# Rotary query products of five quads of heads: seven half-size block products in place of eight full ones

## The reference, cut to what matters

```
q = (x @ wq).reshape(b, s, H, QH)          # H = 16, QH = 128 + 64
q_nope, q_pe = (q[..., :NOPE], q[..., NOPE:])
q_pe = _rope(q_pe, cos, sin)               # 64 columns a head
scores = einsum(concat(q_nope, q_pe), concat(k_nope, k_pe)) * scale, causal
attn = softmax(scores);  out = attn @ v @ wo
```

## Time and profile before

| | us |
|---|---|
| median of 3 runs | 1493.23 (1492.83 to 1495.04) |
| the profiled execution, its own time | 1490.77 |
| its span in the profile | 1489.0 |
| PE busy | 1458.8 (98%) |
| DVE / ACT / POOL busy | 1036.4 / 1013.8 / 1039.1 |

### The profile page before, as it was taken

How to read it: one execution, slowest core, us unless ns; L and a number is a source line. 1 busy time by engine, 2 the same in 40 slices (tenths; PEclk the granted TensorE clock), 3 DMA queues, 4 the chain that set the end, 5 groups by cost and what they waited for, 6 DMA issues and landing times.

```text
span 1489.0 us, 27368 instructions
## 1 busy us (share of the span) xinstructions
PE 1458.8 (98%) x8340; PEld 794.8 (53%) x8340; DVE 1036.4 (70%) x2627; ACT 1013.8 (68%) x2581; POOL 1039.1 (70%) x1087
## 2 busy tenths in 40 slices
PE   6999999999999999999999999999999999999998
PEld 5544555554555545555555555555555555555664
DVE  7877787877777766665656565656656666676887
ACT  7877778777877586667556676666656666654664
POOL 3689787876776588676658866567656876674664
PEclk9999999999999999999999999999999999999999
DMA  6599989898888588787958777886785787864664
GB/s 203 150 195 206 209 185 199 191 187 165 160 172 166 129 155 188 137 190 144 202 109 154 154 137 148 167 158 151 162 194 110 141 163 154 154 160 105 149 146 111
DMA packets 652257, 240.53 MB, mean 162 GB/s; under 512 B 599889, under 2 KB 614737, under 8 KB 651729
## 3 DMA queue, kind: packets, MB, share of 16 engines
q1 hardware_dynamic: 652112, 238.79, 77.3%
HBM read 75.10 MB, written 20.97 MB: 65 GB/s over the span
## 4 chain that ended last, share of the span: by engine, by line
PE 88%; ACT 3%; DVE 3%; POOL 3%; issue 2%; DMA 1%; SPq 0%; POOLq 0%; DVEq 0%; ACTq 0%
PE ps L642 17%; PE ps L644 17%; PE ps L643 17%; PE ps L846 7%; PE ps L852 7%; PE ps L851 7%; PE ps L847 7%; PE ps L848 7%; POOL st L1899 2%; ACT ex L1131 1%; DVE ps L1553 1%; ACT st L1141 0%; DMA acc<-x_in 0%; PE ps L675 0%; DVE acc L1604 0%
## 5 line engine op out<-in xcount | busy, mean ns | idle before, releaser
L1899 POOL TENSOR_TENSOR st<-ex,st 128x512 f16<-128x512 f32 (+3 forms) x640 | 638.3, 1018 | 376.0 <-ACT st L1141 367.8
L1131 ACT ACTIVATE ex<-ps,nm,scales 128x512 f32<-128x512 f32 (+3 forms) x640 | 453.0, 711 | 400.6 <-DVE nm L1570 391.2
L1551 DVE TENSOR_REDUCE gm<-ps 128x1 f32<-128x512 f32 (+1 forms) x384 | 250.3, 671 | 193.8 <-PE ps L852 188.9
L1141 ACT ACTIVATE st<-ex 128x512 f16<-128x512 f32 (+3 forms) x640 | 343.1, 563 | 5.4 <-ACT ex L1131 0.4
L846 PE MATMUL ps<-kTh,q 128*128 128x512 f16 (+3 forms) x640 | 222.3, 347 | 6.9 <-ACT ex L1131 4.3
L642 PE MATMUL ps<-pT,vH 128*128 128x512 f16 (+3 forms) x640 | 222.1, 347 | 1.7 <-DMA pT<-st 1.7
L1604 DVE SCALAR_TENSOR_TENSOR acc<-ps,rden,acc 128x512 f32<-128x512 f32 x256 | 189.6, 745 | 46.8 <-PE ps L644 45.9
L851 PE MATMUL ps<-kRh,q 128*128 128x512 f16 (+3 forms) x640 | 222.2, 347 | 0.0
L852 PE MATMUL ps<-kRl,q 128*128 128x512 f16 (+3 forms) x640 | 222.1, 347 | 0.0
L848 PE MATMUL ps<-kTh,q 128*128 128x512 f16 (+3 forms) x640 | 222.1, 347 | 0.0
L847 PE MATMUL ps<-kTl,q 128*128 128x512 f16 (+3 forms) x640 | 222.1, 347 | 0.0
(11 more groups left out here) (320 smaller groups left out, 2486.6 us busy)
## 6 DMA issues: line engine op xcount, KB each, us to landing
wS<-w_abs SPq DMA_DIRECT2D x48, 256.0 KB, 3.2
wV<-w_vo SPq DMA_DIRECT2D x48, 256.0 KB, 2.9
pT<-st SPq DMA_TRANSPOSE x640, 3.3
wS<-w_abs SPq DMA_DIRECT2D x24, 384.0 KB, 3.4
fland<-factors_in SPq DMA_DIRECT2D x28, 256.0 KB, 3.0
wP<-w_pe SPq DMA_DIRECT2D x24, 256.0 KB, 3.2
wsq<-wq_in SPq DMA_DIRECT2D x16, 256.0 KB, 3.8
wso<-wo_in SPq DMA_DIRECT2D x16, 256.0 KB, 3.1
```

Source lines behind the costliest of these rows:

```text
L1131: e.activation(ex[:, n % NEX, 0:keys], s_bank(n)[:, 0:keys], ACT.Exp, bias=nm[:, (i * QT + r) % 4:(i * QT + r) % 4 + 1], scale=scales[:, p ...
L1141: e.activation(stage(n, keys)[:, :, 0, :], ex[:, n % NEX, 0:keys].rearrange("p (t n) -> p t n", n=P), ACT.Copy).then_inc(z["a_pH"], 1)
L1551: e.tensor_reduce(m, b, AX_X, ALU.max).then_inc(z["v_max"], 1)
L1899: e.tensor_tensor(s[:, :, 1, :], ex[:, n % NEX, 0:keys].rearrange("p (t n) -> p t n", n=P), s[:, :, 0, :], ALU.subtract).then_inc(z["g_pL" ...
```

## The change

The rotary products of the twenty units 28 to 47 (five quads of heads, `QUADS` = 28, 32, 36, 40, 44) are no longer made pair by pair. For a quad, a 512-feature by 256-column weight and a 512-token chunk make a product of two-by-two blocks of 256, and that is done by seven block products: `r1`, `r6`, `r2`, `r5`, `r7`, `r3`, `r4`. Each is two times three matmuls of 256 columns into half a PSUM bank. VectorE reads each bank alone, once or twice, into sums in fp32 that stand in the free part of `pT` (`rope_read`, eight instructions a quad), and `rot` then reads these sums in place of a PSUM bank. The sums and differences of token blocks are those that the non-rotary products already use. The weights' sums are made from the stored weights `w_pe` on GpSimd (14 instructions) and ScalarE (4), once for each of four groups of heads, in nine slots each from (17, 2), (19, 2), (26, 1) and (28, 2) on; they are stored to a new DRAM tensor `w_quad` and loaded for each quad. The products of a quad that begins at unit e stand in slots (e - 6, 0), (e - 6, 2), (e - 6, 3), (e - 4, 0), (e - 4, 2), (e - 4, 3) and (e - 3, 3). `rot` moves from (e - 2, 0) to (e - 3, 2). Units under 28 and from 48 on keep their products as they were. Several of VectorE's semaphores are merged into one, `v_own`, to make room for new ones.

```diff
+FIRST_QUAD = H + 12
+LAST_PASS = (NC - 1) * H
+QUADS = tuple(range(FIRST_QUAD, LAST_PASS, 4))
+R_STEPS = ("r1", "r6", "r2", "r5", "r7", "r3", "r4")
+R_READS = ("s1", "u", "c11", "v", "c22", "u2", "c12", "c21")
+R_LAST = {"r1": "s1", "r6": "u", "r2": "c11", "r5": "v", "r7": "u2", "r3": "c12", "r4": "c21"}
+R_BLOCK = {"r1": (0, 0), "r2": (0, 1), "r6": (2, 1), "r5": (2, 0), "r3": (2, 3), "r7": (2, 2), "r4": (1, 0)}
...
+def quad_slots(e):
+    u = e - 6
+    return {"r1": (u, 0), "r6": (u, 2), "r2": (u, 3), "r5": (u + 2, 0), "r7": (u + 2, 2), "r3": (u + 2, 3), "r4": (u + 3, 3)}
...
+R_SUMMED = tuple(e % H // 4 for e in QUADS[:4])
+R_SUMS = {}
+for n, first in enumerate(((H + 1, 2), (H + 3, 2), (H + 10, 1), (H + 12, 2))):
+    R_SUMS[n] = [divmod(first[0] * 4 + first[1] + s, 4) for s in range(9)]
+R_LOADS = ((H + 1, 0), (H + 3, 0), (H + 8, 0), (H + 11, 3))
+G_SUMS, A_SUMS = 6 * (H // 2), 4 * (H // 2)
...
+def rot_at(x):
+    return (x - 3, 2) if by_quad(x) else (x - 2, 0 if x <= LAST_PASS else 3)
+def turn_at(x):
+    return (x - 2, 2) if x <= (NC - 1) * H else (x - 1, 0)
...
+    rotary = [(step, e) for e in QUADS for step, at in quad_slots(e).items() if at == (i, r)]
...
-        if H <= i <= (NC - 1) * H - 2 and i % 2 == 0:
-            out.append(("pe", i + 2))
+        if i % 2 == 0 and (H < i + 2 < FIRST_QUAD or i + 2 == LAST_PASS):
+            out += rotary + [("pe", i + 2)]
+        else:
+            out += rotary
...
+    if r:
+        out += rotary
...
-IN_BANKS = ("q", "pe", "tkv", "wvo", "tq", "wabs", "out", "ffn", "m1", "m2", "m7")
+IN_BANKS = ("q", "pe", "tkv", "wvo", "tq", "wabs", "out", "ffn", "m1", "m2", "m7") + R_STEPS
...
+            def rope_block(step, x):
+                n, k = QUADS.index(x), x // H
+                o = free_bank((step, x))
+                load = {"r1": "d_ra", "r6": "d_rs", "r4": "d_rb"}
+                if step in load:
+                    e.wait_ge(z[load[step]], 16 * (n + 1))
+                if x % H == 0 and step == "r1":
+                    e.wait_ge(z["d_xT"], 32 * k)
+                if x % H == 0 and step in ("r6", "r7", "r4"):
+                    e.wait_ge(z["g_tok"], 4 * k - 2 + ("r6", "r7", "r4").index(step))
+                part, at = R_BLOCK[step]
+                w = w_quad[part] if part == 1 else w_quad[part][:, at, :, :]
+                token = {"r1": (0, 0), "r2": (1, 0), "r3": (1, 1)}
+                for m in range(2):
+                    rhs = [token_block(k, a, *token[step])[:, m, :] if step in token else
+                           summed(k, {"r6": 2, "r5": 1, "r7": 3, "r4": 4}[step], a)[:, m, :] for a in range(2)]
+                    ins = three(o[:, 0:HC], [w[:, a, m * P:(m + 1) * P] for a in range(2)], rhs, m == 0, m == 1)
+                ins.then_inc(z["p_r"], 1)
...
+            def rope_sums_high(n, step):
+                s, f, ops = {2: (0, 0, 3), 3: (1, 1, 5), 5: (3, 2, 8), 7: (2, 0, 12)}[step]
+                e.wait_ge(z["g_sum"], G_SUMS + 14 * n + ops)
+                if step == 2:
+                    e.wait_ge(z["g_tok"], 4 if n < 2 else 8)
+                    if n:
+                        e.wait_ge(z["d_sS"], 16 * (H // 2 + n))
+                e.activation(r_made[:, s, 0, :], r_tmp[f], ACT.Copy).then_inc(z["a_sum"], 1)
...
+            def rope_read(step, x):
+                c11, c12 = rope_of[0][:, 0:HC], rope_of[0][:, HC:CH]
+                c21, c22 = rope_of[1][:, 0:HC], rope_of[1][:, HC:CH]
+                o = bank((step, x))[:, 0:HC]
+                e.wait_ge(z["p_r"], made_r(step, x))
+                if step == "r1":
+                    if x == FIRST_QUAD:
+                        e.wait_ge(z["p_pv"], H)
+                    e.tensor_copy(c11, o).then_inc(z["v_r"], 1)
+                    return
+                for to, add, behind in {"r6": ((rope_u, c11, "s1"),), "r2": ((c11, c11, "s1"),), "r5": ((c12, rope_u, "u"),),
+                                        "r7": ((c22, c12, "v"), (c21, rope_u, "u")), "r3": ((c12, c12, "v"),),
+                                        "r4": ((c21, c21, "u2"),)}[step]:
+                    e.wait_ge(z["v_r"], read_r(behind, x))
+                    e.tensor_tensor(to, o, add, ALU.add).then_inc(z["v_r"], 1)
...
-                b = bank(("pe", i))
+                if not by_quad(i):
+                    b = bank(("pe", i))
+                    e.wait_ge(z["p_pe"], pe_number(i) + 1)
+                else:
+                    b = rope_of[i % 4 // 2]
+                    e.wait_ge(z["v_r"], read_r("c21" if i % 4 else "c12", i - i % 4))
...
+            def rope_sums(n, step):
+                t0, t1, t2 = r_tmp
+                elif step == 4:
+                    put(t2, h12, t1, sub, behind=5)
+                    put(t2, t2, l12, add, behind=7)
+                    put(r_made[:, 1, 1, :], t1, r_made[:, 1, 0, :], sub, high=2)
...
+            def load_rope(kind, x):
+                n, q = QUADS.index(x), x % H // 4
+                left = {"ra": "r2", "rs": "r3", "rb": "r4"}[kind]
+                if n:
+                    e.wait_ge(z["p_r"], made_r(left, x - 4))
+                else:
+                    e.wait_ge(z["p_pv"], H - 1)
+                if kind == "ra":
+                    e.dma_start(w_quad[0].rearrange("p b a n -> p a b n"),
+                                wP_d[2 * q].rearrange("p a (b n) -> p a b n", b=2)).then_inc(z["d_ra"], 16)
+                elif kind == "rb":
+                    e.dma_start(w_quad[1], wP_d[2 * q + 1, :, :, HC:CH]).then_inc(z["d_rb"], 16)
+                else:
+                    if n < H // 4:
+                        e.wait_ge(z["d_sS"], 16 * (H // 2 + n + 1))
+                    e.dma_start(w_quad[2], wR_d[q]).then_inc(z["d_rs"], 16)
...
-                    if r == (2 if i < H else 0) and i % 2 and H <= i + 3 < NU:
+                    if r == (2 if i < H else 0) and i % 2 and H <= i + 3 < NU and not by_quad(i + 3):
                         load_pe(i + 3)
-                    if r == 1 and h == H - 3 and k + 1 < NC:
+                    for n in R_SUMS:
+                        if (i, r) == R_LOADS[n]:
+                            load_pairs(n)
+                        if (i, r) == R_SUMS[n][-1]:
+                            store_rope_sums(n)
+                    for lead in QUADS:
+                        for kind, at in (("ra", (lead - 9, 0)), ("rs", (lead - 7, 0)), ("rb", (lead - 6, 1))):
+                            if (i, r) == at:
+                                load_rope(kind, lead)
```

More of the change, by code:

```diff
@@ L275, in fills @@
             out += [("pe", e), ("rot", e), ("turn", e)]
-        if H < e <= (NC - 1) * H and (i, r) == (e - 2, 0):
+        if e > H and (i, r) == rot_at(e):
+            if e > LAST_PASS:
+                out += [("den", i - 1)] * (i > LAST_PASS) + [("pe", e)]
             out.append(("rot", e))
[L278 to L282, removed]
+        if e > H and (i, r) == turn_at(e):
             out.append(("turn", e))
@@ L326, in fills @@
         out.append(("wf", KEPT.index((i, r))))
+    for n in R_SUMS:
+        out += [("rsum", (n, s)) for s in range(9) if R_SUMS[n][s] == (i, r)]
     for k in range(1, NC):
@@ L507, in build @@
         wP_d = nc.dram_tensor("w_pe", [H // 2, P, 2, E], F16).ap()
+        wR_d = nc.dram_tensor("w_quad", [H // 4, P, 4, 2, HC], F16).ap()
         xT_d = nc.dram_tensor("x_t", [NC - 1, P, 2 * KE, CH], F16).ap()
@@ L651, in left @@
                 user = used_before[key]
-                if user and user[0] == "s":
+                if user and user[0] in R_LAST:
+                    e.wait_ge(z["v_r"], read_r(R_LAST[user[0]], user[1]))
+                elif user and user[0] == "s":
                     e.wait_ge(z["a_exp"], user[1] + 1)
@@ L1280, in _ @@
         def _(e):
[L1281 removed]
+            chained, made = itertools.count(1), {}
             def own():
@@ L1788, in sums_low, with put @@
                 e.tensor_tensor(weight_block(at, 1), f, weight_block(at, 0), ALU.subtract).then_inc(z["g_sum"], 1)
+            def rope_sums(n, step):
+                t0, t1, t2 = r_tmp
+                (h11, l11), (h12, l12) = [[pair_a[:, b, a, :] for a in range(2)] for b in range(2)]
+                (h21, l21), (h22, l22) = [[pair_b[b][:, a, :] for a in range(2)] for b in range(2)]
+                add, sub = ALU.add, ALU.subtract
+                def put(to, f, g, op, behind=0, high=0):
+                    if behind:
+                        e.wait_ge(z["g_sum"], G_SUMS + 14 * n + behind)
+                    if high:
+                        e.wait_ge(z["a_sum"], A_SUMS + 4 * n + high)
+                    e.tensor_tensor(to, f, g, op).then_inc(z["g_sum"], 1)
+                if step == 0:
+                    e.wait_ge(z["d_rp"], 48 * (n + 1))
+                    if n:
+                        e.wait_ge(z["g_sum"], G_SUMS + 14 * n)
+                    if n == 0:
+                        e.wait_ge(z["p_tkv"], H + 3)
+                        e.wait_ge(z["p_wvo"], H)
```

(22 more changed lines are left out.)

99 lines of the change are left out of this document (77 added, 22 removed).

## The result

The changed kernel is slower: 1498.18 us in the median (1497.44 to 1499.79, 6 runs) against 1492.87 us of the kernel before in the same session; the ratio is 1.0038, 95% interval 1.0025 to 1.0051. The forecast was 1490.1 us, 0.2% faster. The profiled execution took 1498.41 us with a span of 1495.4, so the span grew by 6.4 us where 3.1 less were forecast.

A forecast was written before the change was run, and what follows sets the result against it. A full TensorE queue was taken as the bound. Matmuls -2.9 us and `m6` -0.2, the rest at 0, sum to -3.1, taking the median from 1493.23 to 1490.1 us; range 1488.4 to 1493.3.

The forecast's parts named there:

- Shorter slots: Slots 0 of units 26 to 44 lose rotary matmuls; exponentials, values and banks still fit: cost 0, bound +1 us.
- The sentence on banks: A block product's bank is asked for again at the earliest by the same slot's `out`, in (22, 0) and (24, 0).
- The matmul term: Five quads: 42 matmuls of 256 columns, 0.1094 us each, replace 24 of 512; 0.58 us a quad, 2.92 saved.
- The term of `m6`: Ahead of `m6`: waits gone in five units, -1.0 us, longer in 19 and 21, +0.8; net -0.2 us.
- VectorE, GpSimd, ScalarE, SyncE at nothing: Added reads, `rot` from SBUF, weights' sums and loads cost 0; upper bounds +3 us for `rot`, +2 for GpSimd, ScalarE, SyncE.
- The slower one by GpSimd: GpSimd late in units 17 to 21 and 26 to 30, TensorE standing in eight slots 0: 1499 us; chance 0.06.
- The rival of the weight loads: The 90 added weight loads cost their 98 ns instead of staying hidden: +8.8 us, 1499 us; chance 0.01.
- The sign named for the profile: In the profile after, PE busy in units 16 to 47 is down by 3 us.

The follow-up runs named there:

- the first: Changed kernel with the output product of slot 0 in even units 26 to 44 moved to slot 1, ahead of that slot's own: 1488.98 us, ratio 0.9983.
- fourth: Kernel of the first experiment with the feed-forward product put ahead of the rotary block in the slots they share: 1487.58 us, ratio 0.9973.
- the sixth: Kernel of the fourth experiment with the weights' sums begun one slot later: 1487.82 us, ratio 0.9979.
- the fifth: Kernel before the change, with the output products of slot 0 in even units 26 to 44 moved to slot 1: 1491.87 us, ratio 1.0003.

## Why the prediction was wrong

**The step that failed is "Shorter slots".** It put the cost of taking 1.93 us out of slot 0 at 0, with a bound of +1, after looking at the exponentials, the values and the banks. The first two were judged rightly, since neither waits; the banks come below. What it never asked is what the next instruction of TensorE itself needs: the output product behind the removed matmuls, whose operand VectorE makes in the same slot. The measured cost is 8.47 us. All that was needed were two rows for each slot, VectorE's read and the start of `out`. The smallest spare of the ten, 0.23 us in (32, 0), was in the trace, and so was the same wait come true in (48, 0), 1.08 us; I had the earlier trace rows with 912.31 in it and took it as the end of a stretch of matmuls rather than as a reader. The odd units' slots were as close (0.2 us) and unharmed, as nothing was taken there.

**The sentence on banks in the same step failed too.** It held that a block product's bank is asked for again at the earliest by `out` in (22, 0) and (24, 0). It looked at who follows a block product, and not at whom the shifted rotation puts behind `out`: +0.87 us in (37, 3).

**The matmul term was right.** Over the whole trace the distance from a matmul of the new blocks to the next start, where nothing is waited for, is 0.1093 us in the mean of 201, at the clock of 1.00; forecast were 0.1094. With the output products in the same places the measured gain is 3.0 us, to about 1.8 either way, which agrees with the 2.92 and the small terms around it. By the Trainium skill's "TensorE: Matmul & The Clock Gate", section "Back-to-back issue gap", the same exchange would lose about 4.8 us, the prediction's estimate from that page. The trace does not agree: the 90 added weight loads are in it, and the matmuls stand 0.109 us apart.

**The term of `m6` was right in its places and nearly in each size**: five waits gone, two of 0.54 where 0.64 were forecast. Summed they give -0.5 us, forecast -0.2.

**VectorE, GpSimd, ScalarE, SyncE at nothing were right in the sum.** `rot` out of SBUF was slower than the lower bound, three groups of VectorE after:

```profile
L1678 DVE TENSOR_TENSOR rot<-pT,tab 64x512 f32<-64x512 f32 x10 | 12.5, 1252 | 0.1
L1677 DVE TENSOR_TENSOR rot<-pT,tab 64x512 f32<-64x512 f32 x10 | 11.9, 1190 | 0.1
L1676 DVE TENSOR_TENSOR rot<-pT,tab 128x512 f32<-128x512 f32 x10 | 7.7, 766 | 0.0
```

Together 3.21 us in the mean, between the bounds of 2.06 and 4.6. The ten differ, from 2.06 to 3.78 us, and five of them take 3.77 or 3.78, more than the 3.19 us of slack: there, and once at 3.37, the next maximum starts with no idle time of VectorE ahead of it. No wait of TensorE came of it, as the step had argued. The timeline shows what goes with the long ones: the four of the thirty instructions with no GpSimd instruction beside them take 0.68 or 0.69 us, and all of over 1 us have GpSimd busy for 0.6 us or more of their time. The run without the weights' sums shows GpSimd's and ScalarE's to cost nothing beyond the two waits of `m6`.

**The rivals.** The slower one by GpSimd named 1499 us and the kernel took 1498, but its mechanism did not happen: GpSimd's and ScalarE's added work taken away gives back only the 0.6 us at `m6`. The rival of the weight loads named 1499 too, and the distance of 0.1093 us speaks against it. That both numbers came near is luck. The rival had the right form, a cover of about 1 us used up in many slots, at the wrong reader. The chance of slower, 0.07, came almost all (0.06) from that one mechanism, since the step for shorter slots had been closed as safe. The sign named for the profile, PE busy in units 16 to 47 down by 3 us, came out at 7.8 (684.5 to 676.7): what lies beyond the matmuls is TensorE waiting.

## What to carry to other kernels

When matmuls are taken out of a full TensorE queue, list the readers in order behind them, the very next instruction first, and for each take the start in the trace less the end of what makes its operand. In each slot, what is removed beyond that slot's spare, less the hand-over (0.10 us here), comes back as a wait; here that gives twenty waits in two kernels to 0.14 us. A slot of the trace of before that already lacks the work to be removed, as (48, 0) does here, shows the wait beforehand. And where products take banks in rotation, a new product changes the bank of every later one: look for the pair in which a slow reader now stands one turn ahead.

## What the runs showed of the hardware that was not expected

In some of the executions TensorE ran at half clock for about 3 us behind idle time of about 2 us near the end. The changed kernel (width; busy PE, PEld, DVE, ACT, POOL; granted clock), then the kernel without the weights' sums at the same place:

```profile
1476.00:1479.00 3.00, 0.88 (x4) 0.22 (x3) 1.34 (x3) 2.15 (x5) 1.68 (x2) 0.95 0.70 136
1479.00:1482.00 3.00, 3.00 (x8) 1.00 (x7) 2.17 (x4) 0.00 (x0) 0.38 (x1) 0.50 0.68 132
```

```profile
1476.00:1479.00 3.00, 0.88 (x6) 0.27 (x5) 1.45 (x3) 2.04 (x5) 1.79 (x2) 1.00 0.68 134
1479.00:1482.00 3.00, 3.00 (x16) 1.30 (x16) 3.00 (x5) 0.00 (x0) 0.27 (x1) 1.00 0.69 135
```

A clock of 0.50 is 1.2 in place of 2.4 GHz; 8 matmuls start in place of 16, at 0.43 us apart. By the distances between starts this costs 1.6 us. In the changed kernel some 0.5 of them are not lost: the kernel without the weights' sums waits so long for a transpose just behind, at 1483.02, and the changed one doesn't. Both had TensorE idle for the same 2.12 us ahead of it. The fall was also in the profiled executions of the first and fourth experiments, behind 2.12 us too, and not in that of the sixth, again with 2.12, nor in those of the kernel before (1.83) and the fifth (1.84). So the same idle time is followed by it or not. The kernel before with its pairs in slot 1 shows it in the middle of the kernel, behind its longest new wait (2.45 us, of which the profile has 2.29 as idle), and there its 1.55 us were lost whole:

```profile
1011.00:1014.00 3.00, 0.71 (x5) 0.34 (x5) 1.40 (x4) 3.00 (x9) 2.72 (x3) 1.00 0.46 87
1014.00:1017.00 3.00, 3.00 (x11) 1.44 (x10) 1.44 (x2) 0.72 (x3) 2.17 (x3) 0.52 0.97 188
```

What decides whether it comes stays open. For the reading of a single profiled execution it means that some 1 to 1.6 us of its span may be this.
